# A vision block on one core: more filler at the start, loads, fills and a weighing moved in the opening, and the last block's end in two halves

## The chip, the cores and the metric

One core of a Trainium2 chip runs one program. The metric is the time of one execution on the device in microseconds, the median of several. Engines are named as in the profile: PE is TensorE (matrix products; PEld its weight loads), DVE is VectorE, ACT is ScalarE, POOL is GpSimd, SP is SyncE, which issues most DMA transfers. A `q` behind a name (PEldq, SPq) is that engine's sequencer.

## The reference

Four images of 64 channels by 64 x 64 pixels go through three steps. All data are float32.

```
y    = relu(batchnorm(conv1x1(x)))             # 64 -> 16 channels
wdyn = conv1x1(y)                              # 16 -> 9: a filter of its own for each pixel
h    = sum over the 9 shifts of shift(x) * wdyn            # reshaped to 4096 tokens of 64
h    = h + attention(layernorm(h))             # one head, width 64, softmax over 4096 keys
n    = layernorm(h)
e    = argmax(n @ router + b)                  # one of 32 experts for each token
h    = h + relu(relu(n @ W1[e] + b1[e]) @ W2[e] + b2[e])   # hidden width 16
```

## The kernel before, in words

**Tiling.** An image's 4096 tokens are four blocks of 1024 (`NQ = 4`), so there are 16 blocks, 0 to 15; `par` is the image's parity in double buffers. A block is eight tiles of 128 tokens. For block n the attention walks 16 groups g; a group is one pair of key tiles. It has a *score* (L789: 16 records, products of keys with the block's queries), an exponential (ACT, L1009, two of 128 x 1024) and a *weighing* (L800: 16 records, products of the exponentials with the keys as values, accumulated in `z_ps`). A float32 product is two records. The usual products use a quarter of the array (64*64 in the profile), four side by side.

**Fills.** What else TensorE does for a block comes in *fills* named `name@block`: `cc` and `cv` the two convolutions (for two blocks at once; ACT drains them at L975 and L982), `xt` the transposes of the normalised rows into keys (L628, drained at L984), `g` the queries (L718, drained at L988), `pz` the attention's end, `yt`, `lg`, `ot`, `hid0` to `hid3`, `o2`, `fin` the experts (L737, L637, L763 and L771, L779). Most of them use one PSUM buffer, `both`, so each waits until the one before is drained. `sum0` to `sum2` and `ln` are VectorE's: the nine taps of a block (L1161 and L1173, three taps for each chunk of filters) and its layernorm, which ends in `keys` (L1130). A table written out by hand says after which group's score a fill stands (`opening_groups` for n = 0, `second_groups`, ..., `last_groups`); group -1 is ahead of the block. All engines walk the same table and leave out what isn't theirs; each is strictly in order. `group` (PE) does the score of group g, then the table's fills, then the weighing of group g - 1.

**The opening.** Keys of the first image come into being while it runs. In stage n = 0 the groups are half of block 0's attention and half of block 1's, over the keys of blocks 0 and 1 (groups 0 to 3 need only xt@0; group 4 on needs xt@1); stage 1 needs xt@2 and xt@3. Block 0's filters are computed straight into PSUM (`tap0` to `tap8`). Those of all other blocks go through DRAM: `cv` is copied to `filters_sb`, SP stores it (L420, `store_filters`), and reads it back spread over the channels' rows, in chunks of three taps (L449, `spread_filters`, two transfers of 384 KB to a chunk) into a ring of two slots and, once, a spare one in `chosen`. A slot must have been used before it is filled again.

**SP's order** in the opening: the first weights, image 1's two parts, block 1's filters stored and chunk 0 spread; then a wait for `asked_first`, which TensorE's sequencer signals behind its branch (L862, `shift_if_needed`: it reads a flag, and in this run goes to the part behind `Else`, L873 to L876); then chunks 1 and 2, block 2's filters, image 2, the rest of the weights, the filters of block 2, the store of blocks 3 and 4, and so on. Images are numbered from 1 here and in the title; the code's `load_image(1, ...)` is image 2.

**Filler.** `warm` (L903) issues products of ones with ones that nobody reads, 128*128. `KEEP_WARM` of them stand just ahead of the branch.

**The end.** Block 15 has no attention behind it. Its `hid0` to `hid3` use separate PSUM places (7, 8, 9, 7). `o2` adds its constant part (L763) and 32 records (L771) into two banks, one for each half of the hidden rows; ACT copies one bank (L956), VectorE adds the other (L1278); `fin` turns the result back in 32 products (L779) and VectorE makes the output of it (`put_out`, L1201, two instructions). SP stores it in two transfers (L407).

Of the kernel before, what the change touches and what calls it, by code (L numbers as in the profile page):

```python
# [18 lines left out]
HH = 2  # L19
# [3 lines left out]
BT = QB // 128  # L23
# [43 lines left out]
NONE = ("sum", "ln", "pow", "z", "ask", "warm", "pre", "out")  # L67
# [5 lines left out]
AT_THE_END |= {f"{name}@{BLOCKS - 1}": k for name, k in (("hid0", 7), ("hid1", 8), ("hid2", 9), ("hid3", 7), ("o2", 8))}  # L73
# [3 lines left out]
WARM_UP, STAY_WARM, KEEP_WARM = 8, 10, 10  # L77
# [23 lines left out]

def begins(n, g):

    return g == 0 or n < 2 and g == HALF
# [100 lines left out]
def vit_block_kernel(nc, x, once, kept, out):  # L205
# [6 lines left out]
    with ExitStack() as ctx:  # L212
# [104 lines left out]
        lower_copied, out_ready = sem("lower_copied"), sem("out_ready")  # L317
        choices_stored, choices_loaded = sem("choices_stored"), sem("choices_loaded")
# [75 lines left out]
        def _(sp):  # L394
# [4 lines left out]
            def store_block(m):  # L399
# [3 lines left out]
                else:  # L403
                    sp.wait_ge(drained[places.of[fin]], places.nth[fin])
                for half in range(HH):
                    rows = out.rearrange("b (c h q t) w -> b q h c (t w)", c=C, h=HH, q=NQ)
                    sp.dma_start(rows[m // NQ, m % NQ, half, :, :],  # L407
                                 out_sb[half * C:(half + 1) * C, m % 2, :, :].rearrange("c t w -> c (t w)")
                                 ).then_inc(out_stored[m % 2], 16)
# [104 lines left out]
            for k in range(2):  # L514
                sp.wait_ge(out_stored[k], 32 * BLOCKS // 2)
# [79 lines left out]
        def _(pe):  # L595
# [44 lines left out]

            def begin_hidden(full):
# [5 lines left out]
            def fill(full):  # L647
# [7 lines left out]
                elif name.startswith("pre"):  # L655
                    begin_hidden(f"hid{name[3:]}@{i}")
                if name.startswith(NONE):
                    return
# [97 lines left out]
                elif name == "o2":  # L756
                    if i == BLOCKS - 1:

                        pe.wait_ge(upper_hidden, 2)
# [5 lines left out]
                    for f in range(FT):  # L765
                        wait_drained(f"hid{f}@{i}")
                        if i == BLOCKS - 1:
                            pe.wait_ge(upper_hidden, f + 1)
# [4 lines left out]
                    last.then_inc(done, 1)  # L773
                else:
                    wait_drained(f"o2@{i}")
                    for j in range(4):
                        for r in range(2):
                            for h in range(2):
                                last = T.matmul(both[rows_of(h), r, j * 64:(j + 1) * 64],  # L779
                                                o2_sb[rows_of(r), j * 128 + h * 64:j * 128 + h * 64 + 64],  # L780
                                                ident[rows_of(r), rows_of(r)], start=True, stop=True)
                    last.then_inc(done, 1)
# [97 lines left out]
            def group(n, g, names):  # L880
# [16 lines left out]
                if n < BLOCKS and 0 < g < PAIRS and not at_once:  # L897
# [14 lines left out]
            warm(KEEP_WARM, 256)  # L912
# [14 lines left out]
        def _(act):  # L927
# [9 lines left out]
            def drain(full):  # L937
# [15 lines left out]
                if name == "o2" and i >= BLOCKS - 2:  # L953
# [130 lines left out]
        def _(dve):  # L1084
# [110 lines left out]
            def put_out(i, experts):  # L1195
# [3 lines left out]
                for r in range(2):  # L1199
                    by_half = [t[:, i % 2].rearrange("p (j r) w -> p j r w", r=2)[:, :, r] for t in (out_sb, h2)]  # L1200
# [4 lines left out]
            def drain(full):  # L1205
# [30 lines left out]
                if name.startswith("hid") and i == BLOCKS - 1:  # L1236
# [3 lines left out]
                    return  # L1240
                if name == "out":
# [16 lines left out]
                elif name == "pz":  # L1258
# [12 lines left out]
                    write_normalised(y_block).then_inc(y_ready, 1)  # L1271
                elif name == "o2":
# [3 lines left out]
                    else:  # L1276
                        dve.wait_ge(lower_copied, i - (BLOCKS - 3))
# [137 lines left out]
```

## Time and profile before

| | |
|---|---|
| median of 3 runs | 1112.26 us (1110.14 to 1114.20) |
| profiled execution | 1112.06 us |
| its span, first to last instruction | 1110.3 us |
| mean granted TensorE clock | 0.994 |
| busy: PE, DVE, ACT, POOL | 1087.4, 527.7, 583.2, 13.2 us |

A timeline's columns are start, duration, engine, line, operation, output<-inputs, type of tile, shapes, count, and in brackets the idle time before it and what ended it. A merged row of several instructions lasts from the first's start to the last's end, so rows of one engine overlap. The clock column of a stretch is the mean of what was granted, 1.00 for 2.4 GHz and 0.50 for 1.2 GHz.

### The profile page before, as it was taken

The page shows a single profiled execution, that of the slowest core. Times are in us where ns is not written, and L with a number is a line of the kernel's source. Part 1 is how long each engine was busy: PE and PEld are TensorE (multiplying, and loading weights), DVE is VectorE, ACT ScalarE, POOL GpSimd, SP SyncE. Part 2 cuts the span into 40 slices and gives each one's busy share as a digit, 9 for nine tenths or more (in the row PEclk, how much of TensorE's full clock was granted, in tenths as well). Part 3 has the DMA queues.
Part 4 walks back from the last instruction along what each step waited for, and adds up shares of the span by engine and source line. Part 5 has one row for each costly group of instructions (what it writes and reads, how often), then busy time and mean ns, then how long its engine had stood idle before and what let it go on. Part 6 is the DMA issues. An engine that isn't in the chain of part 4 may idle for free.

```text
span 1110.3 us, 28800 instructions
## 1 busy us (share of the span) xinstructions
PE 1087.4 (98%) x12516; PEld 560.2 (50%) x12516; DVE 527.7 (48%) x1039; ACT 583.2 (53%) x657; POOL 13.2 (1%) x44
## 2 busy tenths in 40 slices
PE   7899999999999999999999999999999999999997
PEld 4244444555444555555555455555545555554543
DVE  7868765436064553735547364553523131312305
ACT  2466656556555464545546465464645545454543
POOL 3100000000000000000000000000000000000000
PEclk9899999999999999999999999999999999999999
DMA  4845621113025140222313023240100101010000
GB/s 107 198 112 131 135 66 35 40 39 78 5 68 119 39 108 20 62 70 68 83 40 91 19 69 80 47 101 11 39 15 11 42 12 41 11 40 3 12 1 20
DMA packets 23057, 63.43 MB, mean 57 GB/s; under 512 B 3934, under 2 KB 8382, under 8 KB 22540
## 3 DMA queue, kind: packets, MB, share of 16 engines
q1 hardware_dynamic: 22364, 61.26, 23.1%
q8 instruction: 103, 1.69, 0.7%
q10 hardware_dynamic: 560, 0.23, 0.1%
q14 instruction: 30, 0.25, 0.1%
HBM read 52.87 MB, written 5.47 MB: 53 GB/s over the span
## 4 chain that ended last, share of the span: by engine, by line
PE 95%; DVE 2%; issue 1%; DMA 1%; ACT 1%; DVEq 0%; PEld 0%; PEldq 0%; SPq 0%
PE z_ps L800 40%; PE scores L789 38%; PE both L637 5%; PE both L771 4%; PE both L628 2%; PE both L779 1%; PE both L737 1%; PE both L718 1%; PE both L728 1%; PE both L697 1%; PE both L685 1%; DMA filter_ring<-filters 1%; PE both L763 0%; PE scores L637 0%; DVE hres L1173 0%
## 5 line engine op out<-in xcount | busy, mean ns | idle before, releaser
L1009 ACT ACTIVATE probs<-scores 128x1024 f32<-128x1024 f32 x512 | 496.4, 1021 | 464.3 <-PE scores L789 464.3
L789 PE MATMUL scores<-g_t,keys_t 64*64 64x512 f32 x4096 | 513.9, 591 | 2.3 <-ACT g_t L988 1.2
L800 PE MATMUL z_ps<-probs,keys 64*64 64x512 f32 x4096 | 510.5, 591 | 0.0
L789 PEld LDWEIGHTS scores<-g_t,keys_t 64*64 64x64 f32 x4096 | 222.3, 134 | 226.7 <-issue 220.7
L800 PEld LDWEIGHTS z_ps<-probs,keys 64*64 64x64 f32 x4096 | 207.4, 133 | 178.9 <-issue 171.8
L1233 DVE SCALAR_TENSOR_TENSOR hidden<-both,chosen 128x1024 f32<-128x1024 f32 x44 | 53.9, 1225 | 200.6 <-PE both L637 189.3
L1173 DVE TENSOR_TENSOR hres<-hres,tap_product 128x504 f32<-128x504 f32 (+1 forms) x128 | 87.8, 686 | 11.2 <-issue 0.9
L1161 DVE SCALAR_TENSOR_TENSOR tap_product<-filter_ring,w,xin 128x504 f32<-128x504 f32 (+1 forms) x117 | 87.0, 743 | 8.1 <-DMA filter_ring<-filters 4.4
L637 PE MATMUL both<-y_t,w 64*64 64x512 f32 x448 | 61.4, 589 | 0.0
L771 PE MATMUL both<-hidden,w 64*64 64x512 f32 x448 | 56.9, 592 | 0.0
L1274 DVE COPY o_sb<-both 128x512 f32<-128x512 f32 x14 | 9.7, 691 | 85.2 <-PE both L771 85.2
L1191 DVE COPY z_sb<-z_ps 128x512 f32<-128x512 f32 x14 | 9.7, 692 | 68.2 <-PE z_ps L800 68.2
L1141 DVE TENSOR_REDUCE stat<-logits 128x8 f32<-128x256 f32 x16 | 6.7, 420 | 64.2 <-ACT logits L994 64.2
L637 PEld LDWEIGHTS both<-y_t,w 64*64 64x64 f32 x448 | 23.4, 133 | 22.4 <-issue 21.7
L771 PEld LDWEIGHTS both<-hidden,w 64*64 64x64 f32 x448 | 24.1, 133 | 20.5 <-issue 19.7
L1262 DVE RECIPROCAL stat<-both 128x8 f32<-128x8 f32 x16 | 3.3, 208 | 57.4 <-PE both L728 57.4
L1121 DVE TENSOR_TENSOR tap_product<-tap_product 128x512 f32<-128x512 f32 x32 | 22.2, 692 | 2.4
L1123 DVE TENSOR_REDUCE stat<-tap_product 128x8 f32<-128x512 f32 x32 | 21.9, 686 | 2.3
L628 PEld LDWEIGHTS both<-w,keys 64*64 64x64 f32 x512 | 11.5, 134 | 14.8 <-issue 14.8
L779 PEld LDWEIGHTS both<-w,o_sb 64*64 64x64 f32 x512 | 13.2, 134 | 9.4 <-issue 9.4
L628 PE MATMUL both<-w,keys 64*64 64x64 f32 x512 | 11.2, 219 | 6.8 <-DVE keys L1130 6.8
L1201 DVE SCALAR_TENSOR_TENSOR out_sb<-both,h 128x256 f32<-128x256 f32 x30 | 11.3, 420 | 13.1 <-PE both L779 13.1
(162 smaller groups left out, 557.5 us busy)
## 6 DMA issues: line engine op xcount, KB each, us to landing
filter_ring<-filters SPq DMA_DIRECT2D x88, 384.0 KB, 5.4
chosen<-choices SPq DMA_DIRECT2D x44, 256.0 KB
out_dram<-out_sb SPq DMA_DIRECT2D x32, 128.0 KB, 2.4
xin<-x_dram SPq DMA_DIRECT2D x6, 528.0 KB, 9.7
g_t<-g_t SPq DMA_DIRECT2D x24, 128.0 KB, 6.1
hidden<-once_dram SPq DMA_DIRECT2D x1, 930.0 KB, 14.4
chosen<-filters SPq DMA_DIRECT2D x2, 384.0 KB, 6.8
choices<-onehot_t SPq DMA_DIRECT2D x22, 32.0 KB, 1.6
```

The costliest lines, as they stand in the source:

```text
L628: last = T.matmul(both[rows_of(a), h, j * 64:(j + 1) * 64], tiles[2 * j + a][rows_of(h)], ident[rows_of(h), rows_of(h)], start=True, stop= ...
L637: last = T.matmul(to[rows_of(c), r, :], weights[rows_of(r), cols], tokens[rows_of(r), :], start=start, stop=stop)
L771: last = T.matmul(mine[rows_of(r), h, :], w2[rows_of(h), f, :], hidden[rows_of(h), f, r, :], start=(f == 0 and h != r), stop=(f == FT - 1))
L779: last = T.matmul(both[rows_of(h), r, j * 64:(j + 1) * 64], o2_sb[rows_of(r), j * 128 + h * 64:j * 128 + h * 64 + 64], ident[rows_of(r), r ...
L789: last = T.matmul(scores[rows_of(h), c, r * 512:(r + 1) * 512], keys_t[rows_of(r), i // NQ % 2, k * 128 + 64 * h:k * 128 + 64 * h + 64], g ...
L800: last = T.matmul(z_ps[rows_of(c), h, :], keys[rows_of(h), i // NQ % 2, 2 * k + r, :], probs[rows_of(h), (2 * g + c) % RING, r * 512:(r + ...
L1009: A.activation(probs[:, unit % RING, :], scores[:, c, :], ACT.Exp, scale=SCALE).then_inc(probs_ready, 1)
L1121: V.tensor_tensor(squares[:, :, :], centred[:, :, :], centred[:, :, :], ALU.mult)
L1123: V.reduce_sum(total, squares[:, :, :], AX_X)
L1161: return V.scalar_tensor_tensor(dst[:, :, lo:hi], flt, keep["b2c"][:, t:t + 1], pix, ALU.add, ALU.mult)
L1173: V.tensor_tensor(mine[:, :, lo:hi], mine[:, :, lo:hi], dst[:, :, lo:hi], ALU.add)
L1233: V.scalar_tensor_tensor(hidden[:, f, :, :], place[k][:, :, :], 0.0, chosen[:, f, :, :], ALU.max, ALU.mult).then_inc(drained[k], 1)
```

## The change

In the opening:

- `KEEP_WARM` is 9 instead of 10, and each product is 512 columns wide instead of 256.
- SP loads image 2 right behind the first weights, ahead of block 1's filters, and spreads chunk 1 together with chunk 0, ahead of the wait for `asked_first`. `store_filters(3)` stands ahead of `spread_filters(2)` instead of behind it.
- cc@3 and cv@3 move from groups 5 and 6 to 1 and 2; cc@5 moves from group 12 to group 3, ahead of xt@1. In group 3 the weighing of group 2 comes between cc@5 and xt@1, and the weighing of group 3 right behind xt@1, so that group 4 has none.

At the end, for block 15 alone:

- The constant part of o2 is a fill of its own (`bias`) ahead of hid3, into `both`.
- o2's products take all 128 rows of `hidden` at once (a 128*64 tile) and 256 tokens each, first all for one half of the tokens, then for the other. No addition of two banks is left: ACT copies the first half, VectorE the second.
- `fin` turns back two tiles of each kind into place 7 behind the first half and two into `both` behind the second. VectorE writes the output in two parts of two instructions each, and SP stores each part in two transfers of half the size.

```diff
-WARM_UP, STAY_WARM, KEEP_WARM = 8, 10, 10
+WARM_UP, STAY_WARM, KEEP_WARM = 8, 10, 9
...
+WAITED = PAIRS // NQ - 1
...
         0: at(1, "sum0 sum1 sum2 ln"),
-        3: at(1, "xt"),
+        1: at(3, "cc"),
+        2: at(3, "cv"),
+        WAITED: [*at(5, "cc"), *at(1, "xt")],
         4: [*at(1, "g"), *at(2, "sum0 sum1 sum2 ln")],
-        5: at(3, "cc"),
-        6: at(3, "cv"),
...
-        12: at(5, "cc"),
...
-                   9: at(m, "hid0 hid1 hid2 hid3"), 10: at(m - 1, "out"), 15: at(m, "o2"), 16: at(m, "fin")})
+                   9: at(m, "hid0 hid1 hid2 bias hid3"), 10: at(m - 1, "out"), 15: at(m, "o2"), 16: at(m, "fin")})
...
             sp.dma_start(w[:, ident_end:], kept[:, ident_end:]).then_inc(kept_loaded, 16)
+            load_image(1, 0, TILES + 2, x_loaded[1])
             store_filters_of(1, 1)
-            spread_filters(1, [0])
+            spread_filters(1, [0, 1])
 
             sp.wait_ge(asked_first, 1)
-            spread_filters(1, [1, 2])
+            spread_filters(1, [2])
             store_filters_of(1, 2)
-            load_image(1, 0, TILES + 2, x_loaded[1])
             sp.dma_start(staged[:, rest_of_it:], once[:, rest_of_it:]).then_inc(once_rest_loaded, 16)
+            store_filters(3)
             spread_filters(2)
-            store_filters(3)
             spread_filters(3)
...
+                parts = 2 if m == BLOCKS - 1 else 1
+                for part in range(parts):
+                    tiles = slice(part * BT // parts, (part + 1) * BT // parts)
+                    if parts > 1:
+                        sp.wait_ge(last_out_ready, part + 1)
...
+            def turn_back(to, first, end):
+
+                for j in range(first, end):
+                    for r in range(2):
+                        for h in range(2):
+                            last = T.matmul(to[rows_of(h), r, j * 64:(j + 1) * 64],
+                                            o2_sb[rows_of(r), j * 128 + h * 64:j * 128 + h * 64 + 64],
+                                            ident[rows_of(r), rows_of(r)], start=True, stop=True)
+                return last
+
+            def begin_last(full):
+
+                wait_free(full)
+                wait_drained(f"ot@{BLOCKS - 1}")
+                for s in range(2):
+                    for part in range(2):
+                        for r in range(2):
+                            T.matmul(both[rows_of(r), s, 0:256], b2_parts[rows_of(r), part, :], onehot_t[rows_of(r), half_of(s)],
+                                     start=(part == 0), stop=False)
+
+            def finish_last(mine):
+
+                for s in range(2):
+                    for f in range(FT):
+                        if s == 0:
+                            wait_drained(f"hid{f}@{BLOCKS - 1}")
+                            pe.wait_ge(upper_hidden, f + 1)
+                        for r in range(2):
+                            last = T.matmul(mine[rows_of(r), s, 0:256], w2[:, f, :], hidden[:, f, r, half_of(s)], start=False,
+                                            stop=(f == FT - 1))
+                    if s == 0:
+                        last.then_inc(lower_ready, 1)
+                return last
...
+                elif i == BLOCKS - 1:
+
+                    pe.wait_ge(upper_hidden, FT)
+                    pe.wait_ge(lower_copied, 2)
+                    turn_back(place[places.of[f"hid3@{i}"]], 0, 2).then_inc(lower_ready, 1)
+                    wait_drained(f"o2@{i}")
+                    turn_back(mine, 2, 4).then_inc(done, 1)
...
                 at_once = n < 2 and g == HALF
-                if at_once:
+                waited = n == 0 and g == WAITED
+                if at_once or waited:
+                    late = names[-1:] if waited else names
+                    for full in names[:-1] if waited else []:
+                        fill(full)
                     usual_weigh(n, g - 1)
+                    for full in late:
+                        fill(full)
+                    if waited:
+                        usual_weigh(n, g)
+                    return
...
-            warm(KEEP_WARM, 256)
+            warm(KEEP_WARM, 512)
...
+                if name == "o2" and i == BLOCKS - 1:
+                    act.wait_ge(lower_ready, 1)
+                    A.copy(o2_sb[:, half_of(0)], both[:, 0, 0:256]).then_inc(lower_copied, 1)
...
+                if full == f"fin@{BLOCKS - 1}":
+                    k = places.of[full]
+                    dve.wait_ge(lower_ready, 2)
+                    put_out(i, place[places.of[f"hid3@{i}"]][:, :, 0:128], 0, 2).then_inc(last_out_ready, 1)
+                    dve.wait_ge(filled[k], places.nth[full])
+                    put_out(i, place[k][:, :, 128:256], 2, 4).then_inc(last_out_ready, 1)
+                    return
...
+                elif name == "o2" and i == BLOCKS - 1:
+                    V.tensor_copy(o2_sb[:, half_of(1)], mine[:, 1, 0:256]).then_inc(done, 1)
```

## Rows read from the trace of the kernel before

**Rows 1.** The page: shares of the chain that ended last, and the exponentials.
```profile
PE 95%; DVE 2%; issue 1%; DMA 1%; ACT 1%; DVEq 0%; PEld 0%; PEldq 0%; SPq 0%
...
L1009 ACT ACTIVATE probs<-scores 128x1024 f32<-128x1024 f32 x512 | 496.4, 1021 | 464.3 <-PE scores L789 464.3
```
**Rows 2.** Stretches: length, each engine's busy time, granted clock, DMA share, GB/s.
```profile
19.00:23.00 4.00, 4.00 (x19) 3.23 (x18) 3.64 (x6) 0.00 (x0) 3.31 (x9) 1.00 0.77 192
23.00:26.80 3.80, 0.07 (x1) 0.00 (x0) 2.93 (x11) 0.00 (x0) 1.47 (x7) 1.00 0.13 33
26.84:31.55 4.71, 2.68 (x41) 0.95 (x41) 3.54 (x5) 1.60 (x2) 0.00 (x0) 0.61 0.94 224
44.20:47.10 2.90, 0.00 (x0) 0.00 (x0) 2.21 (x9) 1.06 (x2) 0.63 (x3) 1.00 0.99 214
47.16:1080.20 1033.04, 1032.27 (x11928) 532.62 (x11928) 475.93 (x925) 558.26 (x620) 2.64 (x3) 1.00 0.22 54
```
**Rows 3.** Chain of waits in order of time, 50 to 60: start, duration, what.
```profile
50.70 2.29 PE scores L789 x16
...
55.56 1.72 PE scores L789 x16
57.28 0.86 PE both L685 x8
```
**Rows 4.** Timeline of TensorE from 18 to 31.
```profile
18.48 4.19 PEld L903 LDWEIGHTS both<-ones 128*128 128x128 f32 x20
...
18.51 4.56 PE L903 MATMUL both<-ones 128*128 128x256 f32 x20
...
28.35 1.98 PE L718 MATMUL both<-keys_t,a_w 64*64 64x512 f32 x8 [0.79 <-ACT keys_t L984]
```
**Rows 5.** Line 862, ahead of 60 and behind it: duration min/median/max in ns.
```profile
L862 PEldq COMPARE_BRANCH  x1: 4811/4811/4811, 20.2 to 20.2; - x1
...
L862 PEldq COMPARE_BRANCH  x3: 323/328/350, 301.3 to 827.0; - x3
```
**Rows 6.** Timeline of VectorE from 30 to 134.
```profile
31.96 0.74 DVE L1161 SCALAR_TENSOR_TENSOR tap_product<-filter_ring,w,xin 128x504 f32<-128x504 f32 x1 [1.27 <-DMA filter_ring<-filters]
...
46.33 0.68 DVE L1130 TENSOR_TENSOR keys<-tap_product,stat 128x504 f32<-128x504 f32 x1
...
73.06 0.75 DVE L1161 SCALAR_TENSOR_TENSOR hres<-filter_ring,w,xin 128x512 f32<-128x512 f32 x1 [4.47 <-DMA filter_ring<-filters]
...
91.81 0.68 DVE L1130 TENSOR_TENSOR keys<-tap_product,stat 128x504 f32<-128x504 f32 x1
...
113.86 0.75 DVE L1161 SCALAR_TENSOR_TENSOR hres<-filter_ring,w,xin 128x512 f32<-128x512 f32 x1 [1.26 <-DMA filter_ring<-filters]
...
132.54 0.68 DVE L1130 TENSOR_TENSOR keys<-tap_product,stat 128x504 f32<-128x504 f32 x1
```
**Rows 7.** Timelines of SyncE and TensorE from 60 to 135.
```profile
63.64 2.15 SPq L420 DMA_DIRECT2D filters<-filters_sb  x4
...
107.87 10.10 SPq L449 DMA_DIRECT2D filter_ring<-filters  x6
...
134.44 0.67 PE L628 MATMUL both<-w,keys 64*64 64x64 f32 x32
```
**Rows 8.** Timeline from 1100 to 1107, the last block's end.
```profile
1100.18 3.63 PE L771 MATMUL scores<-hidden,w 64*64 64x512 f32 x30
...
1103.86 0.59 ACT L956 COPY o_sb<-scores 128x512 f32<-128x512 f32 x1 [3.25 <-PE scores L771]
1104.55 0.69 DVE L1278 TENSOR_TENSOR o_sb<-o_sb,scores 128x512 f32<-128x512 f32 x1 [3.18 <-ACT o_sb L956]
...
1105.38 0.70 PE L779 MATMUL both<-w,o_sb 64*64 64x64 f32 x32 [1.57 <-DVE o_sb L1278]
1106.13 0.76 DVE L1201 SCALAR_TENSOR_TENSOR out_sb<-both,h 128x256 f32<-128x256 f32 x2 [0.90 <-PE both L779]
```
**Rows 9.** Line 407 behind 1080: duration min/median/max in ns, first and last start.
```profile
L407 SPq DMA_DIRECT2D out_dram<-out_sb x4: 466/532/597, 1101.4 to 1107.4; - x4
```

More of the change, by code:

```diff
@@ L59 @@
 KEPT_AT, KEPT_N = columns(KEPT)
-NONE = ("sum", "ln", "pow", "z", "ask", "warm", "pre", "out")
+NONE = ("sum", "ln", "pow", "z", "ask", "warm", "pre", "out", "bias")
 CHOSEN_BY_DMA = range(3, BLOCKS - 2)
@@ L72 @@
 AT_THE_END = {f"{name}@{BLOCKS - 2}": k for name, k in (("hid0", 7), ("hid1", 8), ("hid2", 7), ("hid3", 8), ("o2", 9))}
-AT_THE_END |= {f"{name}@{BLOCKS - 1}": k for name, k in (("hid0", 7), ("hid1", 8), ("hid2", 9), ("hid3", 7), ("o2", 8))}
+AT_THE_END |= {f"{name}@{BLOCKS - 1}": k for name, k in (("hid0", 7), ("hid1", 8), ("hid2", 9), ("hid3", 7), ("o2", 0), ("fin", 8))}
 AHEAD = tuple(f"hid{f}@{BLOCKS - 1}" for f in range(FT - 1))
 PLACES = 10
-WARM_UP, STAY_WARM, KEEP_WARM = 8, 10, 10
+WARM_UP, STAY_WARM, KEEP_WARM = 8, 10, 9
 CHUNK = 3
@@ L402, in store_block @@
                     sp.wait_ge(out_ready, 1)
-                else:
+                elif m < BLOCKS - 2:
                     sp.wait_ge(drained[places.of[fin]], places.nth[fin])
[L405 to L409, printed above, removed]
+                parts = 2 if m == BLOCKS - 1 else 1
[3 more added lines that the diff above has]
+                        sp.wait_ge(last_out_ready, part + 1)
+                    for half in range(HH):
+                        rows = out.rearrange("b (c h q t) w -> b q h c t w", c=C, h=HH, q=NQ)[m // NQ, m % NQ, half, :, tiles]
+                        sp.dma_start(rows.rearrange("c t w -> c (t w)"),
+                                     out_sb[half * C:(half + 1) * C, m % 2, tiles, :].rearrange("c t w -> c (t w)")
+                                     ).then_inc(out_stored[m % 2], 16)
             def store_filters(i):
@@ L656, in fill @@
                     begin_hidden(f"hid{name[3:]}@{i}")
+                elif name == "bias":
+                    begin_last(f"o2@{i}")
                 if name.startswith(NONE):
@@ L757, in fill @@
                     if i == BLOCKS - 1:
-                        pe.wait_ge(upper_hidden, 2)
+                        finish_last(mine).then_inc(done, 1)
+                        return
                     for part in range(2):
@@ L773, in fill @@
                     last.then_inc(done, 1)
+                elif i == BLOCKS - 1:
[4 more added lines that the diff above has]
+                    turn_back(mine, 2, 4).then_inc(done, 1)
                 else:
                     wait_drained(f"o2@{i}")
[L776 to L782, printed above, removed]
+                    turn_back(both, 0, 4).then_inc(done, 1)
             def score(n, g, c):
@@ L892, in group @@
                 at_once = n < 2 and g == HALF
-                if at_once:
-                    usual_weigh(n, g - 1)
+                waited = n == 0 and g == WAITED
[3 more added lines that the diff above has]
+                        fill(full)
+                    usual_weigh(n, g - 1)
+                    for full in late:
[3 more added lines that the diff above has]
+                    return
                 for full in names:
                     fill(full)
-                if n < BLOCKS and 0 < g < PAIRS and not at_once:
+                if n < BLOCKS and 0 < g < PAIRS and not (n == 0 and g == WAITED + 1):
                     usual_weigh(n, g - 1)
@@ L952, in drain @@
                     A.copy(conv1[:, :, 0:256], both[:, :, 0:256]).then_inc(drained[k], 1)
-                if name == "o2" and i >= BLOCKS - 2:
+                if name == "o2" and i == BLOCKS - 2:
                     k = places.of[full]
@@ L1193, in whole_z, with put_out @@
                     V.tensor_tensor(z_sb[:, :], z_sb[:, :], z_ps[:, 1, :], ALU.add).then_inc(z_copied, 1)
-            def put_out(i, experts):
+            def put_out(i, experts, first=0, end=BT // 2):
                 if i > 1:
@@ L1199, in put_out @@
                 for r in range(2):
-                    by_half = [t[:, i % 2].rearrange("p (j r) w -> p j r w", r=2)[:, :, r] for t in (out_sb, h2)]
+                    by_half = [t[:, i % 2].rearrange("p (j r) w -> p j r w", r=2)[:, first:end, r] for t in (out_sb, h2)]
                     last = V.scalar_tensor_tensor(by_half[0], experts[:, r].rearrange("p (j w) -> p j w", w=D), 0.0,
```

8 lines of the change are left out of this document (4 added, 4 removed).

## The prediction

> **What bounds the kernel now.** I read the chain of waits first. TensorE holds 95% of it [rows 1], so the end moves only if TensorE loses work or idle time, or if the ends of the run, where it isn't the bound, get shorter. The stretches show where that can be. From the 47th microsecond to the 1080th TensorE is never idle; in the opening it is idle for 3.7 of 3.8 us around the 25th and for all 2.9 us before the 47th, and behind the first the granted clock is at its lower level, 1.2 of 2.4 GHz, for most of the next 4.7 us (mean 0.61) [rows 2]. Behind the second the slow clock shows in the chain: group 4's score takes 2.29 us where the later one takes 1.72 [rows 3]. The second gap is VectorE's: it ends when xt@1 gets block 1's normalised rows, and VectorE itself waited 1.27 us for filter chunk 1 on the way there [rows 4, 6]. The end of the run is a string of handovers between engines [rows 8]. So I cost three things: the two gaps, the work put into them, and the last string.
>
> **The longer products.** 20 records of 256 columns took 4.56 us [rows 4]. A record of 512 columns holds the array 0.43 us (16 records of a quarter of the array each, four side by side, take 1.72 [rows 3]), so the 18 new ones end at 18.5 + 7.7 = 26.2, where the old ones ended at 23.1. xt@0 waits for the keys until 26.84. Whether the filler delays it depends on the branch behind it: TensorE's sequencer met the branch at 20.2, while the filler was still running, and it took 4.81 us, until 25.05; the same branch later in the run took 0.33 [rows 5]. So the filler isn't in the branch's way: the branch runs beneath it.
>
> **Filter chunk 1 and image 2 sooner.** Image 2's two transfers go out behind the first weights and ahead of block 1's filters, which are stored and fetched back by 18.1; cc@3 wants them after 34, so I cost them at nothing. Without that cover cc@3, and TensorE behind it, would wait for them as (e) says. Chunk 1 follows chunk 0 at 18.1 instead of waiting for the branch. It then lands before VectorE's 30.7, which takes the 1.27 us wait away [rows 6]: keys@1 are done at 45.7 instead of 47.0. The price is on TensorE. The long branch ended 2 us after the DMA engines had moved chunk 0 (share 0.77 up to 23.0, 0.13 behind it [rows 2]), which is what one sees if its code came in behind chunk 0. Two transfers of 384 KB at the 224 GB/s of the next stretch [rows 2] are 3.4 us more in that queue. Bounds for the end of the branch: 25.05 (code doesn't queue behind data) and 28.45 (it queues behind all of it). I take the upper end, because the branches later in the run, with no bulk ahead of them, are so short; xt@0 starts at 28.6, 1.75 us later than now. Chunk 2, asked for after the branch, is issued at 28.5 and needs 6.0 us, as chunk 0 of block 5 did from 107.87 to 113.86 [rows 6, 7]: 34.5. VectorE wants it one chunk behind 30.7, three products of 0.74 [rows 6] and three sums of nearly that, at 35.1.
> The Trainium skill (Runtime: NRT & Kernel Launch, Instruction fetch mechanics) says that a taken branch out of the pages that are loaded has to fetch its page by DMA first. The 4.81 us against 0.33 agree; the page gives no time for a loaded queue, so it doesn't choose between my two bounds.
>
> **Four fills and a weighing moved.** With g_t of block 0 there, TensorE now does scores 0 to 3, weighings 0 and 1, and waits; the change puts cc@3 and cv@3 into groups 1 and 2 and cc@5 and weighing 2 ahead of xt@1, and weighing 3 behind it. That is 3 x 0.86 + 1.72 = 4.3 us of work out of the full stretch [rows 3]. Does the gap hold it? Eight records take 0.86 us at full clock [rows 3] and twice that at the lower level, which g's 1.98 were [rows 4]; so scores start 4.71 - 0.9 = 3.8 us behind xt@0 [rows 2]: at 30.6 if the branch is early, 32.4 if it is late. Up to xt@1 stand four scores, three weighings and three fills, 7 x 1.72 + 3 x 0.86 = 14.6 us, and 0.4 because the second score waits for the first exponentials (1.02 each [rows 1], against 0.86 for half a score): 45.6 or 47.4. So early or late, there is no gap any more, and no slow clock after it. xt@1 (0.46) and weighing 3 end at 48.0 or 49.6. To compare, the kernel before has xt@1, weighings 2 and 3, scores 4 and g@1 done at 55.56 [rows 3]. The new one reaches the same, with three fills (2.6 us) more done, at 50.6 or 52.2. TensorE alone would gain 55.56 + 2.58 - 50.6 = 7.5, or 5.9 us.
>
> **What is late next: VectorE's blocks 2 to 5.** xt@5 starts at 134.44 and its keys were done at 133.22 [rows 6, 7]: only 1.2 us of slack, 1.07 behind the handover. So what counts is how far VectorE comes forward. SP now does store_filters(3) ahead of spread_filters(2), so block 2's chunks are queued behind the drain of cv@3. I follow it for the early branch: scores 0 to 2, cc@3, weighing 0 and cv@3 are 8.6 us and 0.4 for the first exponentials, so cv@3 is computed at 39.6; ScalarE copies it, in 1.0 us like an exponential of the same shape [rows 1] and behind one, 40.8; four issues take 2.15 [rows 7]; the chunk takes 6.0: block 2 starts at 49.0. A block takes 92.49 - 73.06 = 19.43 us [rows 6]: keys@2 at 68.4. There the gain comes: block 3 waited 4.47 us for its filters because cv@3 came so late [rows 6], and now they are there. keys@3 at 68.4 + 0.1 + 19.5 = 88.0, against 92.49. From there to keys@5 all is driven by VectorE and by the transfers that it releases (image 3 and the stores of cv@5 go out behind block 4's last chunk, block 5's first chunk is issued at 107.87 and waited for [rows 6, 7]), so I carry the 40.7 us from 92.49 to 133.22 over: keys@5 at 128.7, xt@5 at 128.85. The opening gains 134.44 - 128.85 = 5.6 us with the early branch and 5.6 - 1.75 = 3.85 us with the late one. VectorE takes some 2 us of what TensorE alone would gain. Behind xt@5 VectorE has slack again.
>
> **The last block in halves.** The first-term products of o2 (0.4 us) move into the pause before hid3, while VectorE drains hid0. The 32 half-width records use all 128 rows and half of the columns each, so two side by side fill the array: 16 x 0.213 = 3.4 us, as many array cycles as the 3.46 now (30 of its 32 records are in [rows 8]). The other end, no two of them side by side, is 6.8 us. I take 3.4: in the old form the two column halves of the same rows already run side by side. They end at 1103.4 instead of 1103.84. Behind them stood ScalarE 0.59, VectorE 0.69, 32 products 0.70, VectorE 0.76 and the handovers: 1106.89 [rows 8]. Now: a copy of 256 columns (at most the 0.42 of one of the two instructions at L1201) 1103.9, 16 products 0.5 and handovers 1104.5, half an output 0.5: 1105.0. But SP issues four stores instead of two, at 0.53 each [rows 9]: from 1104.5, when the first part is there, the last one starts no sooner than 1106.2, against 1107.4 [rows 9]. The gain is 1.2 us (up to 1.9 if the stores don't bind).
> For the weights of these products a rule of the Trainium skill (TensorE: Matmul & The Clock Gate, The mechanism) speaks against the change: a weight load runs beneath a running product only where their row groups differ, and here they never do. By it 16 pairs with a load of 0.21 (4.19 / 20 [rows 4]) in front would take 16 x 0.42 = 6.8 us and the tail would lose 2.2. The fillers show otherwise: their 20 loads on all rows are busy for 4.19 us inside the 4.56 us of products that alone take 20 x 0.213 = 4.3 [rows 4].
>
> **Sum.** 3.85 + 1.2 = 5.05 us off. The profiled execution took 1112.06 us (span 1110.3 and 1.8 around it), 0.2 under the median of 1112.26: 1107.0.
>
> **Rivals.**
> (a) The early branch: code doesn't wait for bulk data. 5.6 + 1.2 = 6.8: 1105.3. For it: the filler covers it wholly, and nothing in the trace times a branch behind a longer queue.
> (b) The clock falls in the opening all the same. TensorE has only xt@0 and g (some 1.6 us of work) between 26.2 and 32. If it falls as it did now, at 0.61 over that stretch [rows 2], the same work costs 0.9 on g and up to 1.9 on the first scores: 2.8 us, which also puts cv@3 and with it VectorE's chain back. With the late branch 1109.8, with the early one 1108.1. The spread of 4 us between the runs of before says that this differs from one run to the next.
> (c) The half-width products don't run side by side, or their loads show: 2.1 to 3.4 us more, 1109.1 to 1110.4.
> (d) SP stands at cv@3. Each microsecond that cv@3 comes late puts block 2's chunks, keys@3 and xt@5 back by as much; the whole gain of 6.8 is gone when it is drained at 47.6 instead of 40.8. That takes a low clock that lasts: late branch, g at half clock (scores from 33.3), 9 us of work at half clock for 17: cv@3 drained near 52, 11 us late, 1116. Against it: the low level ended by itself after the first scores.
> (e) The moved fills wait for what they need (image 2, the drain of `both`) and nothing is won but the tail: 1110.9.
>
> **How the numbers follow.** Forecast 0.35, (a) 0.24, (b) 0.24, (c) 0.08, (d) 0.05, (e) 0.04. A measurement of this kernel tells some 0.3%, 3.3 us, from no change, so faster means below 1108.9. Forecast, (a) and half of (b): 0.71. The rest of (b), (c) and (e): 0.24. (d): 0.05. The range reaches from 1104.7, (a) with the stores not binding, to 1110.4, the far end of (c); it leaves out (d), (e) and little else.
>
> **What would show it.** The branch's record at the same line: under 5 us for (a), near 8 for the forecast; xt@0 at 26.9 or 28.6. The granted clock from 27 to 36: full, or (b). No idle TensorE before xt@1. cv@3 drained near 42.5, block 2's first product near 50.8, no wait before block 3's, keys@5 near 130.5 and xt@5 right behind it. In the tail: o2's records in 3.4 us, and four stores back to back. The prediction fails if xt@5 isn't where TensorE waits, or if block 2 starts much later than 51.

## The result, and the profile after

| | before | after |
|---|---|---|
| median of 18 runs each | 1113.34 us | 1107.89 us |
| fastest and slowest | 1110.14, 1116.87 | 1106.36, 1110.61 |
| profiled execution, its span | 1112.06, 1110.3 | 1107.86, 1106.1 |

The ratio is 0.9950, with a 95% interval of 0.9941 to 0.9959: 5.6 us faster (4.6 to 6.6). 1107.0 was predicted, from a time before of 1112.26 us, so that the forecast's gain of 5.05 us is the number to compare. The two profiled executions are 4.2 us apart.

The page after: span, busy time of each engine, shares of the chain that ended last ([rows 1] before).

```profile
span 1106.1 us, 28808 instructions
...
PE 1090.9 (99%) x12518; PEld 557.3 (50%) x12518; DVE 527.0 (48%) x1041; ACT 582.9 (53%) x657; POOL 13.3 (1%) x44
...
PE 91%; DVE 3%; DMA 2%; ACT 1%; issue 1%; DVEq 1%; SPq 0%; ACTq 0%
```

The chain now runs through DMA and VectorE for a good part of the opening, from 43.5 to 110.8: those are the shares that TensorE lost. It begins with the drain of cv@3, goes on with the store and the load of block 2's filters, and ends in the keys of block 4 (start, duration, what):

```profile
43.46 0.91 ACT filters_sb L1041
...
45.42 0.86 DMA filters<-filters_sb
46.32 5.25 DMA filter_ring<-filters
51.68 0.75 DVE hres L1220
```

Stretches of the opening after (length, busy time of PE, PEld, DVE, ACT, POOL, granted clock, DMA share, GB/s), beside [rows 2]:

```profile
17.50:18.50 1.00, 0.48 (x4) 0.25 (x3) 1.00 (x2) 0.62 (x3) 0.00 (x0) 1.00 0.11 21
18.70:22.10 3.40, 3.40 (x6) 1.73 (x7) 3.07 (x5) 0.16 (x1) 2.18 (x8) 0.51 0.77 182
22.10:32.30 10.20, 8.19 (x59) 3.42 (x61) 8.72 (x20) 1.60 (x2) 2.54 (x8) 1.00 0.83 195
32.30:35.80 3.50, 3.50 (x20) 1.24 (x23) 3.26 (x6) 1.02 (x1) 0.00 (x0) 0.52 0.60 230
35.80:48.90 13.10, 12.84 (x122) 4.19 (x113) 8.91 (x20) 9.93 (x10) 3.78 (x5) 1.00 0.18 45
```

TensorE has no long gap any more up to xt@1, so both gaps of [rows 2] are filled; what is left is the 2 us in which it waits for ScalarE ahead of g and of the first score. But the clock was at its lower level twice, from 18.7 to 22.1 beneath the new filler, behind a stretch in which TensorE had worked for half of the time, and from 32.3 to 35.8 beneath the first scores. The lines that answer to [rows 4] and [rows 5], the filler, xt@0, g and the branch:

```profile
18.94 9.50 PE L959 MATMUL both<-ones 128*128 128x512 f32 x18
...
28.38 0.69 PE L640 MATMUL both<-w,keys 64*64 64x64 f32 x32
...
29.87 1.09 PE L766 MATMUL both<-keys_t,a_w 64*64 64x512 f32 x8 [0.80 <-ACT keys_t L1043]
...
L909 PEldq COMPARE_BRANCH  x1: 5721/5721/5721, 20.5 to 20.5; - x1
```

VectorE's line that answers to [rows 6], and the two transposes that answer to [rows 7]:

```profile
51.68 0.75 DVE L1220 SCALAR_TENSOR_TENSOR hres<-filter_ring,w,xin 128x512 f32<-128x512 f32 x1 [5.67 <-DMA filter_ring<-filters]
...
70.48 0.68 DVE L1189 TENSOR_TENSOR keys<-tap_product,stat 128x504 f32<-128x504 f32 x1
...
89.64 0.68 DVE L1189 TENSOR_TENSOR keys<-tap_product,stat 128x504 f32<-128x504 f32 x1
...
110.78 0.68 DVE L1189 TENSOR_TENSOR keys<-tap_product,stat 128x504 f32<-128x504 f32 x1
...
130.75 0.68 DVE L1189 TENSOR_TENSOR keys<-tap_product,stat 128x504 f32<-128x504 f32 x1
...
111.61 0.69 PE L640 MATMUL both<-w,keys 64*64 64x64 f32 x32 [0.95 <-DVE keys L1189]
...
131.59 0.69 PE L640 MATMUL both<-w,keys 64*64 64x64 f32 x32
```

VectorE stood idle for 5.67 us ahead of block 2, and TensorE waited for keys once, 0.95 us at xt@4; xt@5 is at 131.59 instead of 134.44. The end after, beside [rows 8]:

```profile
1097.07 3.67 PE L681 MATMUL both<-hidden,w 128*64 128x256 f32 x32
...
1099.06 0.37 ACT L1015 COPY o_sb<-both 128x256 f32<-128x256 f32 x1 [1.26 <-PE both L681]
...
1100.79 0.42 DVE L1339 COPY o_sb<-both 128x256 f32<-128x256 f32 x1 [2.23 <-PE both L681]
1101.20 1.09 DVE L1260 SCALAR_TENSOR_TENSOR out_sb<-scores,h 128x128 f32<-128x128 f32 x4
```

The last output is written at 1102.29, 4.6 us sooner than before; 2.85 of these are the opening's.

### The profile page after: what moved, and what is told of

Its sections match the earlier page's. It is cut to its first block, busy times and chain, and to the rows that moved or that the text cites. A ratio compares the mean times of both kernels' runs of the same rounds, so it can differ in the third digit from the quotient of the medians.

```text
span 1106.1 us, 28808 instructions
## 1 busy us (share of the span) xinstructions
PE 1090.9 (99%) x12518; PEld 557.3 (50%) x12518; DVE 527.0 (48%) x1041; ACT 582.9 (53%) x657; POOL 13.3 (1%) x44
## 4 chain that ended last, share of the span: by engine, by line
PE 91%; DVE 3%; DMA 2%; ACT 1%; issue 1%; DVEq 1%; SPq 0%; ACTq 0%
PE z_ps L847 37%; PE scores L836 36%; PE both L649 5%; PE both L817 4%; DMA filter_ring<-filters 2%; PE both L640 1%; PE both L959 1%; PE both L658 1%; DVE hres L1232 1%; DVEq L1148 1%; PE both L785 1%; PE both L776 1%; PE both L766 1%; PE both L733 1%; PE both L811 0%
## 5 line engine op out<-in xcount | busy, mean ns | idle before, releaser
L776 PEld LDWEIGHTS both<-wv_w,z_sb 64*64 64x64 f32 x512 | 12.7, 134 | 8.5 <-issue 8.5
L959 PE MATMUL both<-ones 128*128 128x128 f32 (+1 forms) x54 | 15.8, 461 | 1.0 <-POOL ones L532 1.0
L785 PEld LDWEIGHTS both<-router_w,y_t 64*64 64x64 f32 x512 | 12.8, 134 | 6.9 <-issue 6.0
```

Of the source, the lines that this page charges most:

```text
L776: last = T.matmul(both[rows_of(h), c, j * 65:(j + 1) * 65], z_sb[rows_of(c), j * 128 + h * 64:j * 128 + h * 64 + 64], wv_w[rows_of(c), c * ...
L785: last = T.matmul(both[rows_of(h), r, j * E:(j + 1) * E], y_t[rows_of(r), j * 128 + h * 64:j * 128 + h * 64 + 64], router_w[rows_of(r), :] ...
L959: T.matmul(both[:, 1, 0:columns], ones[:, :], ones[:, :].unsqueeze(1).broadcast_to([128, columns // 128, 128]), start=True, stop=True)
```

## The experiments

All are edits of the changed kernel unless said otherwise. Three sets ran, each with runs of the kernel before beside it, and "against" in a result names that set's median of it. Ratios compare with the runs of the same set, too, so two sets are best compared by their ratios. Diffs are against the changed kernel.

### Set 1: the two halves, the filler, and SP's order

**opening_only** is the kernel before with every edit of the opening, **tail_only** the one with every edit of the end.

> The kernel before with all of the opening's edits and the old end. Theory: the opening and the end are independent, and the opening carries the larger part. The profiled pair has it at 134.44 - 131.59 = 2.9 us up to xt@5, but both profiled executions had a slow clock in the opening; over many runs I expect 4.2 us off the kernel before (ratio 0.9962). Rival, the end carries more than its 1.3 us: then this one is only 2 to 3 us faster (0.9978).

Measured: 1108.26 against 1113.12, ratio 0.9959 (0.9946 to 0.9971), 4.6 us.

> The kernel before with the edits of the last block's end alone. Theory: 1.3 us off the kernel before (ratio 0.9988); the 32 half-width records take about 3.5 us and four stores back to back set the end. Rival, the products on all 128 rows don't run side by side or their loads show: 0.9 to 2 us slower than before. The profile after has them at 3.67, so I hold that for unlikely.

Measured: 1111.45 against 1113.12, ratio 0.9981 (0.9970 to 0.9992), 2.1 us (0.9 to 3.3). Together they make the 5.6 us of the change within their intervals, and the opening carries the larger part. In the profile of opening_only TensorE waited for keys at xt@4 (1.23 us) and at xt@5 (0.65 us). The profiles tell the end's share more closely: from the end of hid3 to the end of the span 10.4 us before (1099.9 to 1110.3) and 9.0 after (1097.1 to 1106.1), 1.4 us.

**short_filler**

```diff
-WARM_UP, STAY_WARM, KEEP_WARM = 8, 10, 9
+WARM_UP, STAY_WARM, KEEP_WARM = 8, 10, 10
...
-            warm(KEEP_WARM, 512)
+            warm(KEEP_WARM, 256)
```

> The changed kernel with the old filler ahead of the branch, 10 products of 256 columns instead of 9 of 512. Theory A, the one of my prediction: the branch (until 26.3 in the profile after) sets xt@0, so a shorter filler makes xt@0 no later; it starts near 26.9, and what the long filler is worth is the clock: with an idle gap of 2 to 3 us ahead of xt@0 the clock is low behind it more often, and this kernel is 1 to 2 us slower than the changed one. Theory B: the long filler itself, at the low clock that it met in the profile after, is what put xt@0 at 28.4; without it everything up to block 2's filters comes 1.5 us sooner and this kernel is up to 1.5 us faster than the changed one. Both: branch record of 5.7 us, as it was.

Measured: 1108.64 against 1113.12, ratio 0.9959 (0.9944 to 0.9973). The changed kernel had 0.9950, and 0.9945 in set 3, so the long filler is worth about 1 us by the medians, which these intervals don't tell from nothing. The profile speaks for theory A on the clock: xt@0 starts as soon as the keys are there, but g and the scores run at half clock.

```profile
27.57 1.13 PE L640 MATMUL both<-w,keys 64*64 64x64 f32 x32 [3.79 <-DVE keys L1189]
29.49 1.99 PE L766 MATMUL both<-keys_t,a_w 64*64 64x512 f32 x8 [0.79 <-ACT keys_t L1043]
32.69 3.69 PE L836 MATMUL scores<-g_t,keys_t 64*64 64x512 f32 x16 [1.22 <-ACT g_t L1047]
```

Scores start at 32.69, no sooner than behind the long filler (32.17), and take twice as long. The branch's record was 5.13, so it ended at 26.0 and held nothing: theory A had the clock right, its price is not clear of noise, and it had the branch wrong. One of the six runs, the one with a mean clock of 0.998 (0.995 in the others), took 1105.63 us, less than any run of the changed kernel; the others took 1107.89 to 1109.39. So the long filler looks like an insurance: it costs time where the clock would have stayed up. One run doesn't show that.

**store3_behind**

```diff
-            store_filters(3)
             spread_filters(2)
+            store_filters(3)
```

> The changed kernel with store_filters(3) behind spread_filters(2), as it was before. Theory: VectorE idled 5.7 us ahead of block 2 because SP stood at cv@3's drain; now block 2's first product starts near 46.2 instead of 51.7, keys@5 come 5 us sooner (near 126.5 instead of 131.4) and no xt waits for its keys; TensorE then loses nothing, which is the 0.95 us that it waited ahead of xt@4, or up to 2 us by my prediction's sum: 1 to 2 us faster than the changed kernel. Rival: block 3's chunks come late again as before (a wait of over 4 us ahead of block 3), which gives the gain back: same as the changed kernel or slower.

Measured: 1105.58 against 1113.12, ratio 0.9937 (0.9926 to 0.9949). Its VectorE from 46 to 128:

```profile
56.52 0.74 DVE L1220 SCALAR_TENSOR_TENSOR tap_product<-filter_ring,w,xin 128x504 f32<-128x504 f32 x1 [0.44 <-DMA filter_ring<-filters]
66.55 0.68 DVE L1189 TENSOR_TENSOR keys<-tap_product,stat 128x504 f32<-128x504 f32 x1
...
127.35 0.68 DVE L1189 TENSOR_TENSOR keys<-tap_product,stat 128x504 f32<-128x504 f32 x1
```

There is no wait ahead of block 2 and none ahead of block 3: cv@3 was drained at 43.2, long before SP came to its store at 52.0. keys@2 come 3.9 us sooner than after, keys@5 3.4 us (I had said 5), and no xt waits.

### Set 2: chunk 1, the moved fills, and filler in the pauses

**chunk1_behind**

```diff
-            spread_filters(1, [0, 1])
+            spread_filters(1, [0])
...
-            spread_filters(1, [2])
+            spread_filters(1, [1, 2])
```

> The changed kernel with filter chunk 1 issued behind TensorE's branch again, beside chunk 2. Theory: the branch's code queues behind the bulk data. With one chunk ahead of it the branch's record was 4.8 and 4.5 us, with two 5.7, 5.1, 7.2 and 5.7; here it comes back to 4.5 to 4.9 us. xt@0 does not move, since the filler and not the branch holds it (28.4 in the profile after), VectorE waits for chunk 1 again for 0.5 to 1.5 us, and xt@1 at 49.0 doesn't notice: same time as the changed kernel within 0.5 us. Rival, my prediction's: the branch sets xt@0, so this kernel starts its scores 1 us or more sooner and is 1 us faster. Rival 2: chunk 1 sooner is worth its 1.3 us on VectorE: this one is 1 us slower.

Measured: 1106.95 against 1112.53, ratio 0.9957 (0.9939 to 0.9974), no different from the changed kernel. The branch took 5.66 us, not the 4.5 to 4.9 that I expected. VectorE waited 2.74 us for chunk 1, where I expected 0.5 to 1.5, and xt@1 did notice:

```profile
33.54 0.74 DVE L1220 SCALAR_TENSOR_TENSOR tap_product<-filter_ring,w,xin 128x504 f32<-128x504 f32 x1 [2.74 <-DMA filter_ring<-filters]
...
48.64 0.69 PE L640 MATMUL both<-w,keys 64*64 64x64 f32 x32 [1.23 <-DVE keys L1189]
...
130.58 0.69 PE L640 MATMUL both<-w,keys 64*64 64x64 f32 x32
```

In the second profile of the changed kernel (after_again, set 3) xt@1 is at 47.27 and xt@5 at 130.21. So a lead of 1.37 us at xt@1 is one of 0.37 at xt@5: what TensorE wins by an early chunk 1 it waits away again at xt@4 (1.45 us in after_again, 0.41 here). That is VectorE as the bound, seen from the other side.

**fills_unmoved** has the table of the opening and the order within a group as before, and store_filters(3) behind spread_filters(2).

```diff
-        1: at(3, "cc"),
-        2: at(3, "cv"),
-        WAITED: [*at(5, "cc"), *at(1, "xt")],
+        3: at(1, "xt"),
         4: [*at(1, "g"), *at(2, "sum0 sum1 sum2 ln")],
+        5: at(3, "cc"),
+        6: at(3, "cv"),
...
+        12: at(5, "cc"),
```

> The changed kernel with cc@3, cv@3, cc@5 and the weighings in their old groups, and store_filters(3) behind spread_filters(2) as then. What is left of the opening's edits is the filler, image 2 and chunk 1 sooner. Theory: the moved work is nearly all of the opening's gain; the gap of TensorE ahead of xt@1 is back (2 to 3 us long, ending near 46.5, where VectorE now is 1.3 us sooner), and a slow clock behind it in most runs: 2 to 2.5 us faster than the kernel before, of which the end's edits are 1.3 to 1.9 (ratio 0.998). Rival, the loads and the filler carry the gain: 4 us faster than before or more.

Measured: 1108.29 against 1112.53, ratio 0.9967 (0.9953 to 0.9981), 3.7 us; I had expected 2.2. The gap is back as expected (2.97 us ahead of xt@1, and a clock of 0.50 in the two microseconds from 48), and so is VectorE's wait for block 3:

```profile
46.56 1.08 PE L641 MATMUL both<-w,keys 64*64 64x64 f32 x32 [2.97 <-DVE keys L1181]
...
72.40 0.75 DVE L1212 SCALAR_TENSOR_TENSOR hres<-filter_ring,w,xin 128x512 f32<-128x512 f32 x1 [4.90 <-DMA filter_ring<-filters]
```

Against store3_behind, which differs from it in the moved work alone, the moved work is worth 2.7 us by the medians (1108.29, 1105.58) and 3.3 by the ratios. What is left of the 3.7 us without the end's 1.4 to 2.1 is some 2 us for the filler and the early loads, which no run here takes apart further than short_filler and chunk1_behind do. "Nearly all" was too much for the moved work.

**pause_filler** and **all_pauses** add products nobody reads to store3_behind.

```diff
+            def warm_z(count, columns):
+
+                for _ in range(count):
+                    T.matmul(z_ps[:, 1, 0:columns], ones[:, :],
+                             ones[:, :].unsqueeze(1).broadcast_to([128, columns // 128, 128]), start=True, stop=True)
...
                 for full in names:
                     fill(full)
+                    if full in ("xt@0", "g@0"):
+                        warm_z(1 if full == "xt@0" else 2, 256)
```

> store3_behind with three more products of 256 columns that nobody reads, into z_ps: one behind xt@0 and two behind g@0, where TensorE waits for ScalarE (0.8 and 1.2 us). Theory: what still differs from run to run is the slow clock behind the thin stretch of xt@0 and g (it held from 32.3 to 35.8 in the profile after); with the pauses filled it doesn't fall there, the spread of the runs shrinks, and the median is 0.3 to 0.8 us under store3_behind. Rival: at the low clock the fillers outlast the pauses and push the scores back by 0.5 us; no gain.

Measured: 1105.60 against 1112.53, ratio 0.9944 (0.9928 to 0.9960): no gain over store3_behind, and no smaller spread (1105.15 to 1106.80, against 1105.08 to 1106.45). Scores already ran at the full clock in the profile of store3_behind (16 records in 1.95 us), so in that execution the pauses had nothing to win.

all_pauses has this besides; the added wait lets VectorE read tap4 out of the bank before the products write there:

```diff
                     power_step(int(name[3:]))
+                    if int(name[3:]) > 1:
+                        for _ in range(2):
+                            T.matmul(z_ps[:, 0, 0:128], ones[:, :], ones[:, :], start=True, stop=True)
+                    elif name == "pow1":
+                        wait_drained("tap4@0")
```

> pause_filler with two products of 128 columns behind each of the small power products from the third on, into z_ps's first bank. Theory: the clock falls at 18.7 to 20.2 in most profiled executions, behind the stretch in which TensorE only does the power products, and makes the long filler last 9.5 us instead of 7.7, so xt@0 starts at 28.4 to 28.9 instead of 26.9. With those pauses filled it stays at the full clock, the filler ends near 26.6, xt@0 starts near 27, and the kernel is 1 to 1.5 us faster than pause_filler. Rival: the added products delay the power products, the flag and the branch by as much as they win.

Measured: 1106.54 against 1112.53, ratio 0.9953 (0.9936 to 0.9970), 0.9 us behind pause_filler by the medians of one chip and not in front of it. The rival holds. The clock never fell (mean 1.000) and the filler took 7.89 us, but it started 1.5 us later than in pause_filler, the branch 1.2 us later, and that one ended at 29.3:

```profile
L914 PEldq COMPARE_BRANCH  x1: 7407/7407/7407, 21.9 to 21.9; - x1
...
20.42 7.89 PE L972 MATMUL both<-ones 128*128 128x512 f32 x18
29.89 0.69 PE L640 MATMUL both<-w,keys 64*64 64x64 f32 x32 [1.58 <-issue]
```

### Set 3: the two orders side by side, a lighter filler, and the branch without bulk ahead

**after_again** is the changed kernel itself, **store3_again** is store3_behind.

> The changed kernel once more, beside the next one on the same chip, for a direct comparison and a second look at where it waits. Theory: 5 to 5.5 us faster than before (ratio 0.995); TensorE waits for the keys at xt@4 or xt@5 for 0.4 to 1.9 us, block 2 starts near 51, the clock is low once at least ahead of 36.

Measured: 1106.79 against 1113.15, ratio 0.9945 (0.9932 to 0.9959).

> store3_behind once more. Theory: 1.5 to 2 us under after_again, with no wait of TensorE for keys from 60 to 140. Rival: the difference seen across the calls (ratios 0.9937 and 0.9950, their intervals overlap) was the chip's: no difference.

Measured: 1105.48 against 1113.15, ratio 0.9933 (0.9920 to 0.9947). The five runs of each on this chip don't overlap (1106.40 to 1107.56, 1105.23 to 1105.96): 1.3 us, near the 0.95 and 1.45 us that TensorE waited at xt@4 in the two profiles of the changed kernel. The fastest version of this study is store3_behind, 0.6 to 0.7% under the kernel before, with pause_filler no different from it.

```profile
50.14 0.75 DVE L1220 SCALAR_TENSOR_TENSOR hres<-filter_ring,w,xin 128x512 f32<-128x512 f32 x1 [4.12 <-DMA filter_ring<-filters]
...
110.38 0.69 PE L640 MATMUL both<-w,keys 64*64 64x64 f32 x32 [1.45 <-DVE keys L1189]
...
109.44 0.65 PE L640 MATMUL both<-w,keys 64*64 64x64 f32 x32
```

The first two lines are after_again's, the third is xt@4 in store3_again, without a wait.

**light_pauses** is store3_behind with half of all_pauses' products at the power steps, none behind xt@0 and g@0, and `KEEP_WARM` 8 of 512 columns.

> store3_behind with one product of 128 columns behind each power product from the third on, and 8 long fillers of 512 columns instead of 9. Theory: in all_pauses the clock never fell, but its extra products put the flag and with it the branch back by 1.3 us and the branch then set xt@0 (29.9). With half as many the branch starts by 21.3 and ends by 27 to 28.5, the filler ends by 27, xt@0 starts there, and the kernel is 0 to 1 us faster than store3_again, no more, because the branch stands where the filler stood. Rival: the filler was what held xt@0 in store3_behind, and this one is 1.5 us faster.

Measured: 1106.92 against 1113.15, ratio 0.9938 (0.9923 to 0.9953), with the widest spread of all, 1104.10 to 1110.88. The ratio is no different from store3_again's, so the gain of 0 to 1 us that I expected isn't shown. In the profiled execution, the slowest, the branch took 8.60 us, TensorE was idle for 3.5 us ahead of xt@0 and the clock was low behind it. I read that as a bet on a short branch; the faster runs have no profile.

**no_bulk_ahead** (one run)

```diff
-            spread_filters(1, [0, 1])
-
             sp.wait_ge(asked_first, 1)
-            spread_filters(1, [2])
+            spread_filters(1)
```

> The changed kernel with no filter chunk ahead of TensorE's branch: chunks 0, 1 and 2 are all issued behind asked_first. Theory: the branch's code queues behind the bulk data, so its record, 4.5 to 5.7 us with one chunk ahead and 5.1 to 7.4 with two, is 3 to 4 us here. VectorE waits for chunk 0 for some 3 us, which costs the opening 2 us or so. Rival: the length of the branch has nothing to do with the chunks; the record stays at 4.5 us or more.

Measured: 1110.43 in the one run against 1113.15, which gives no interval. The branch:

```profile
L907 PEldq COMPARE_BRANCH  x1: 3752/3752/3752, 20.8 to 20.8; - x1
```

With the bulk behind it the branch is at its shortest, and VectorE waited 5.04 us for chunk 0, more than the 3 us that I expected. Ordered by what was issued ahead of it, the records are 3.8 us (no chunk), 4.5, 4.8 and 5.7 (one: tail_only, before, chunk1_behind), and 5.1 to 8.6 (two, in ten profiled executions: 5.1, 5.2, 5.4, 5.7, 5.7, 7.2, 7.3, 7.4, 7.4 and 8.6). The bulk ahead lengthens the branch; by how much differs from run to run.

The traces show more than the lengths. In each of the 14 profiled executions one packet of some 16 KB in queue q8, which the page calls an instruction queue, moves while the branch is waiting, and the branch's record ends 2.4 to 3.0 us behind the start of that packet. What varies is when the packet comes: 1.0 us behind the start of the branch with no chunk ahead, 2.1 to 2.9 us with one, 2.5 to 5.9 us with two. So the part of the branch that differs is that packet's wait. The trace doesn't say for which engine the packet is, and what decides its place among the bulk data is open: in five of the ten executions with two chunks it moved at 23.0 to 23.6, in the middle of them, in the others at 25.1 or later.

## Why the prediction was right

**The sum.** 5.05 us were predicted and 5.6 (4.6 to 6.6) measured; 3.85 for the opening against 4.6 (opening_only) and 2.85 in the profiled pair, 1.2 for the end against 1.4 by the profiles. The range holds. That the opening's term came out so close is in part luck, as the next two steps show.

**The longer products: a step that failed.** "The 18 new ones end at 26.2" took the full clock for granted, because the kernel before had it there [rows 4]. They ended at 28.4 after, and in all but store3_again and no_bulk_ahead of the other profiled kernels with nine long products and the old power steps they also met the low clock (9.67 us instead of 7.97). Even the old filler met it once: 6.25 us in tail_only instead of 4.56. The power products ahead of the filler leave TensorE half idle (0.48 of 1.00 us from 17.5 to 18.5). That this brings the clock down is likely and not shown: with these products the clock fell in 8 of 12 profiled executions, with the pauses filled (all_pauses, light_pauses) in neither of two. I looked for a fall of the clock only behind the filler, as rival (b), and it was ahead of it as well.

**The branch: right size of the delay, wrong cause.** I let the branch set xt@0, at 28.6. xt@0 was at 28.38, but the branch had ended at 26.2, between my bounds of 25.05 and 28.45, and the slow filler held xt@0. Two errors cancelled each other, which is luck. In opening_only, fills_unmoved and pause_filler the branch did end near my upper bound, at 28.0 to 28.1, and xt@0 began 0.6 to 0.7 us behind it. That is the same distance as in all_pauses and light_pauses, where the filler was over and the branch alone held xt@0; in the first three the late branch and the slow filler came out alike. That the code queues behind bulk data is borne out by no_bulk_ahead and by the packets of q8; that it waits for all of it holds in some executions and not in others. The Trainium skill's rule (Runtime: NRT & Kernel Launch, Instruction fetch mechanics) agrees with these traces, since even with no chunk ahead the branch took 3.75 us and a packet of instructions moved meanwhile. What the chunks ahead add is taken from the runs alone.

**Rival (b) came true in part.** The clock fell behind xt@0 and g in the profiled execution, from 32.3 to 35.8, for half as long as before (27.9 to 34.8). It didn't in after_again. This is much of the spread between runs: the slowest run after had a mean clock of 0.994, the fastest 0.999.

**The moved work: right.** No gap ahead of xt@1 (12.84 of 13.10 us busy up to 48.9), and no low clock behind it. Worth 2.7 to 3.3 us in SP's old order; in the change it came with the new order, which takes 1.3 us of that back.

**VectorE next: right mechanism, its price too high.** Block 2 began at 51.7 and 50.1 (predicted 50.8) and took 19.5 us in the first profile (19.43), no wait ahead of block 3, keys@5 at 131.4 and 130.1 (130.5), TensorE waiting for keys. But TensorE lost 0.95 to 1.45 us by it in the two profiles of the changed kernel and not 2, and undoing SP's order gave 1.3 back; in opening_only it lost 1.88. The term that was mis-sized in the profiled pair is the time of TensorE alone, which took the full clock all the way: xt@1 came at 49.0 and not at 47.4, and a TensorE that is itself late waits less for keys. In after_again xt@1 came at 47.27, as reckoned; there block 2's filters were 0.7 us earlier than reckoned, and the wait was 1.45 us. I also named xt@5 as the place; the wait was at xt@4, and only in opening_only at xt@5 too. And I took SP's new order as a necessity of the change and priced it only against block 3's old 4.47 us. The other order was to be had: with cv@3 drained at 43.2 in store3_behind it cost nothing.

**The end: right.** The half-width products run side by side: 3.67 us for 32, predicted 3.4, and 6.8 was the other end. By the rule of the Trainium skill (TensorE: Matmul & The Clock Gate, The mechanism) that loads run beneath products only of other row groups, they would have needed 6.8 too, though the same section also lets a load into a background weight buffer go ahead. This case's trace is against the rule without that exception, twice: in the fillers, and here with 32 loads of 3.22 us inside the 3.67. Of the 1.75 us that the shorter string saves up to the last output SP's four stores take some 0.35 back in all.

**Chunk 1 sooner** took VectorE's 1.27 us wait away, as predicted, and was worth nothing measurable (chunk1_behind), since VectorE then waited for block 2 instead. With store3_behind's order there is no such wait, and there a late chunk 1 wasn't tried.

## What to carry to other kernels

When work is moved into a gap, follow the queue entries that are moved along with it: here SP's wait for a drained fill moved ahead of the next loads, and cost the engine that became the bound 4 to 6 us of idle time, 1.3 us of the whole; swapping two lines gave it back. Filler ahead of a branch can cover the wait for its code, here 5.7 us of it, and bulk transfers issued just ahead of the branch made it longer and less certain (3.8 us without, 5.1 to 8.6 with two chunks). A product that only keeps the clock up is itself at the mercy of the clock: look at what the engine did before it.

## What the runs showed that I had not expected

The same branch took 3.8 to 8.6 us depending on what was issued ahead of it and on the run, and nearly all of the difference is the time until one packet of instructions moves. And 18 filler records of 512 columns took 7.97 us at the full clock and 9.67 when 3.4 us of them ran at the lower level, behind a stretch that small products of 65 rows filled by half; in two of nine executions with the same products ahead the clock stayed up.
